# MLP: incoming items are normalised on ScalarE by scale and shift, and the first four are added and measured one by one

## The reference

```
x = x + attention_part(layernorm(x))
h0 = layernorm(x)                       # the incoming item, normalised: no weight, no bias
for blk in range(3):
    y = qlora_linear(h, first weights)
    y = gelu(layernorm(y) * gamma + beta)
    y = qlora_linear(y, second weights)
    h = y + h
x = x + h
```

## Time and profile before

| | |
|---|---|
| median of 3 runs | 1937.06 us (1936.43 to 1937.8) |
| profiled execution, its own time | 1935.07 us |
| its span | 1933.3 us |
| its mean TensorE clock | 0.972 of full speed |
| PE busy | 1806.9 us (93%) |
| DVE busy | 1434.5 us (74%) |
| ACT busy | 1311.9 us (68%) |
| POOL busy | 1184.4 us (61%) |
| `mlp_items` begins (first add, L1681) | 1526.6 us |

### The profile page before, as it was taken

How to read it: one execution, slowest core, us unless ns; L and a number is a source line. 1 busy time by engine, 2 the same in 40 slices (tenths; PEclk the granted TensorE clock), 3 DMA queues, 4 the chain that set the end, 5 groups by cost and what they waited for, 6 DMA issues and landing times. The chain is left out here.

```text
span 1933.3 us, 36509 instructions
## 1 busy us (share of the span) xinstructions
PE 1806.9 (93%) x12544; PEld 1375.2 (71%) x12544; DVE 1434.5 (74%) x3135; ACT 1311.9 (68%) x2317; POOL 1184.4 (61%) x1032
## 2 busy tenths in 40 slices
PE   5799999999999999999999999999995699999998
PEld 4577777766777777777776777777763478888887
DVE  4687778887878777777777777777762677777865
ACT  2777776677777775777677776777751177777775
POOL 2466666666666664555555555555542088888886
PEclk9899999999999998999999999999997599999999
DMA  4011111111111111111111111111012311212001
GB/s 144 23 39 39 39 38 38 49 55 43 41 40 38 38 39 39 39 39 39 44 53 51 38 43 38 38 38 38 27 35 69 109 66 42 90 45 88 23 23 45
DMA packets 87272, 91.97 MB, mean 48 GB/s; under 512 B 4928, under 2 KB 82448, under 8 KB 87184
## 3 DMA queue, kind: packets, MB, share of 16 engines
q1 hardware_dynamic: 79360, 79.46, 12.6%
q10 hardware_dynamic: 7824, 11.37, 2.4%
HBM read 57.26 MB, written 25.17 MB: 43 GB/s over the span
## 5 line engine op out<-in xcount | busy, mean ns | idle before, releaser
L860 POOL TENSOR_TENSOR L_xc<-L_xpad,L_vec 128x512 f32<-128x512 f32 x160 | 166.2, 1039 | 421.3 <-ACT L_xpad L659 394.1
L381 PE MATMUL L_front<-L_uhi,L_whi 128*128 128x512 f32 x576 | 247.3, 429 | 13.1 <-DVE L_xc L1078 8.3
L530 PE MATMUL L_mix<-L_wo,L_yg 128*128 128x256 f32 x1024 | 238.4, 387 | 3.2 <-POOL L_yg L852 3.2
L381 PE MATMUL L_front<-L_uhi,L_wlo 128*128 128x512 f32 x576 | 229.7, 399 | 0.0
L381 PE MATMUL L_front<-L_ulo,L_whi 128*128 128x512 f32 x576 | 229.6, 399 | 0.0
L1090 DVE TENSOR_TENSOR L_m<-L_dbank,L_gm 128x512 f32<-128x512 f32 x256 | 175.7, 687 | 69.3 <-ACT L_dbank L699 68.8
L852 POOL TENSOR_TENSOR L_yg<-L_yg,L_sz 128x512 f32<-128x512 f32 x128 | 164.2, 1283 | 85.9 <-DVE L_yg L1105 85.9
L530 PEld LDWEIGHTS L_mix<-L_wo,L_yg 128*128 128x128 f32 x1024 | 191.8, 192 | 34.7 <-issue 7.0
L659 ACT ACTIVATE L_xpad<-L_front,L_pbias 128x512 f32<-128x512 f32 x160 | 108.8, 681 | 132.4 <-PE L_front L381 131.6
L697 ACT ACTIVATE L_dbank<-L_dbank 128x512 f32<-128x512 f32 x256 | 148.8, 581 | 45.1 <-PE L_dbank L437 45.0
L487 PE MATMUL L_ybank<-L_m,L_dtx 128*64 128x128 f32 x2048 | 161.3, 284 | 5.5 <-DVE L_m L1090 5.4
(11 more groups left out here) (172 smaller groups left out, 4683.3 us busy)
## 6 DMA issues: line engine op xcount, KB each, us to landing
h<-L_hres SPq DMA_DIRECT2D x32, 512.0 KB, 3.0
L_hin<-in_x SPq DMA_DIRECT2D x16, 512.0 KB, 4.7
L_hres<-in_x SPq DMA_DIRECT2D x16, 512.0 KB, 3.9
L_cc<-L_xc ACTq DMA_DIRECT2D x64, 128.0 KB, 2.3
L_hin<-h SPq DMA_DIRECT2D x16, 512.0 KB, 4.7
L_hres<-h SPq DMA_DIRECT2D x16, 512.0 KB, 3.8
M_hin<-h SPq DMA_DIRECT2D x16, 512.0 KB, 4.6
M_xin<-in_x SPq DMA_DIRECT2D x16, 512.0 KB, 5.6
```

The costliest lines, as they stand in the source:

```text
L381: last = nc.tensor.matmul(to[:, :], ww[:, kd, tile * P:(tile + 1) * P], a[:, kd, :], start=i == 0, stop=i == len(passes) - 1)
L530: last = nc.tensor.matmul(mix[1 - s][:, (b % 2) * DM:(b % 2 + 1) * DM], yg[:, t, b * P:(b + 1) * P], wo[layer][:, t, :], start=t == 0, sto ...
L860: nc.gpsimd.tensor_tensor(xc[p][:, q, :].rearrange("p (b i) -> p b i", b=NB), xpad[:, q, :, 0:P], vector(layer, "conv_w", q * TAPS, 1).uns ...
```

## The change

`norm_in` leaves DVE for ACT. It no longer computes (v - mean) * rstd but v * rstd + shift0, so DVE makes -mean (`mean0`, one more 128x4 instruction in `in_moments`), and POOL makes shift0 (one more 128x4 instruction in `scale_in`). On ACT an item's four tiles are done in two halves, in two successive steps, right ahead of the gelu; PE waits for both halves. `scale_in` moves behind `block_scale` in POOL's step. The first four items are now added, measured and scaled one item a step, in steps -4 to -1, and normalised in steps -2 to 1. For later items the steps of `add_x`, `in_stats`, `in_moments` and `scale_in` are as before (3, 5, ... and 4, 6, ...), and `norm_in` stands at 6 and 7, 8 and 9, 10 and 11, 12 and 13.

```diff
+        mean0, shift0 = sb("mean0_", [P, NB]), sb("shift0_", [P, NB, 1])
...
 (PE, turn_in)
-                pe.wait_ge(n0_done, t + 1)
+                pe.wait_ge(n0_done, 2 * t + 2)
...
 (ACT)
+            def norm_in(t, half):
+                if t is None:
+                    return
+                u = t % UNITS
+                act.wait_ge(n0_shift, t + 1)
+                for b in (2 * half, 2 * half + 1):
+                    last = nc.scalar.activation(normed[u][:, b, :], held_by(t)[:, b, :], ACT.Identity, bias=shift0[u][:, b, :], scale=rstd0[u][:, b, :])
+                last.then_inc(n0_done, 1)
...
                 round_h(n, 1)
+                norm_in(entering(n, 2, 6), 0)
+                norm_in(entering(n, 2, 7), 1)
                 gelu(n - 2, 0)
...
 (POOL, scale_in)
                 nc.gpsimd.tensor_tensor(rstd0[u][:, :, 0], var0[u][:, :, 0], power[:, :], ALU.pow).then_inc(n0_rstd, 1)
+                pool.wait_ge(n0_rstd, t + 1)
+                pool.wait_ge(n0_mean, t + 1)
+                nc.gpsimd.tensor_tensor(shift0[u][:, :, 0], mean0[u][:, :], rstd0[u][:, :, 0], ALU.mult).then_inc(n0_shift, 1)
...
                 rest_h(n + 1, 1)
-                scale_in(entering(n, 2, 4))
                 block_scale(n)
+                scale_in(entering(n, 4, 4))
...
 (DVE, in_moments)
                 nc.vector.tensor_scalar(var0[u][:, :, 0], mv0[u][:, :, 1], EPS, None, ALU.add).then_inc(n0_var, 1)
-
-            def norm_in(t):
-                if t is None:
-                    return
-                u = t % UNITS
-                dve.wait_ge(n0_rstd, t + 1)
-                dve.wait_ge(n0_mom, NB * t + NB)
-                for b in range(NB):
-                    last = nc.vector.tensor_scalar(normed[u][:, b, :], held_by(t)[:, b, :], mv0[u][:, b, 0:1], rstd0[u][:, b, :],
-                                                   ALU.subtract, ALU.mult)
-                last.then_inc(n0_done, 1)
+                nc.vector.tensor_scalar(mean0[u][:, :], mv0[u][:, :, 0], -1.0, None, ALU.mult).then_inc(n0_mean, 1)
...
 (DVE, step)
-                norm_in(entering(n, 1, 5))
-                add_x(entering(n, 7, 3))
-                in_stats(entering(n, 2, 4), 0)
+                add_x(entering(n, 4, 3))
+                in_stats(entering(n, 4, 4), 0)
...
-                in_moments(entering(n, 2, 4))
+                in_moments(entering(n, 4, 4))
                 block_stats(n, 3)
```

More of the change, by code:

```diff
@@ L1422, in mlp_items @@
         b_mean, b_normed = sem("b_mean"), sem("b_normed")
+        n0_mean, n0_shift = sem("n0_mean"), sem("n0_shift")
         b_turned, b_gelu, g_hi, g_lo = (sem(n) for n in ("b_turned", "b_gelu", "g_hi", "g_lo"))
@@ L1750, in step @@
                 add_h(n - 3, 1)
-                norm_in(entering(n, 1, 5))
-                add_x(entering(n, 7, 3))
-                in_stats(entering(n, 2, 4), 0)
-                in_stats(entering(n, 2, 4), 1)
+                add_x(entering(n, 4, 3))
+                in_stats(entering(n, 4, 4), 0)
+                in_stats(entering(n, 4, 4), 1)
                 add_out(n - 3, 0)
@@ L1757, in step @@
                 block_stats(n, 0)
-                in_stats(entering(n, 2, 4), 2)
+                in_stats(entering(n, 4, 4), 2)
                 block_stats(n, 1)
-                in_stats(entering(n, 2, 4), 3)
+                in_stats(entering(n, 4, 4), 3)
                 block_stats(n, 2)
-                in_moments(entering(n, 2, 4))
+                in_moments(entering(n, 4, 4))
                 block_stats(n, 3)
```

## The result

The changed kernel takes 1941.12 us (median of 16 runs, 1937.96 to 1942.41) where the kernel before took 1934.62 us (16 runs, 1932.63 to 1939.13). The ratio is 1.0029, 95% interval 1.0021 to 1.0036: slower by 0.3%. I had forecast 1935.3 us and a range of 1927 to 1939; the time lies above the range. The forecast stood on the median of three runs, 1937.06 us; against the 16 runs its change of -1.8 us would be 1932.8 us, and the measured change is +6.5 us. The profiled execution has a span of 1939.9 us, 6.6 us more than before, at a mean clock of 0.971 (before 0.972).

A forecast was written before the change was run, and what follows sets the result against it. PE was taken as the bound, losing time to POOL's late low part of the gelu. Rounds -0.6 and start -1.2 gave -1.8 us, so 1935.3 us; range 1927 to 1939, leaving out 2 in 10.

The forecast's parts named there:

- The blocked mean: On DVE, `mean0` behind `var0` waits 1.27 us for POOL's second `rest_h`, delaying the slot's statistics and `var`.
- POOL's wait for the slot's `var`: On POOL, before the slot's power in steps 4, 6, 8, 10: idles about 1.1 us.
- `add_x` now falls on the new power, which lets it pass; only the small shift behind it waits, some 0.2 us instead of 1.0: DVE's add runs beside the incoming item's power on POOL; only shift0 is delayed, some 0.2 us.
- 0.2 to 0.4 behind `add_x`: Term in POOL's time for two steps: its waiting behind DVE's add, 0.2 to 0.4 us.
- the pair's sum: POOL's time for two steps: slots' work, item's power, shift0, idling and waiting behind `add_x`, 15.1 us against 15.61 before.
- the forecast of the rounds: Three rounds of entering items: PE loses 3.4 us each instead of 3.6, together -0.6 us.
- the path to PE: PE's `turn_normed` follows POOL's `rest_g` by about 0.4 us, so step 5 begins 1.1 us late.
- the power holds off `add_x`: Slower rival: `add_x` waits for the incoming power's end, +1.0 us on POOL in nine steps; +7, 1944 us; chance 0.06.
- "-1.2 us" at the start: First four items: slot 0's normalise begins 1.0 + 0.15 us earlier and ACT carries that on, -1.2 us.
- 0 if item 1's shift is held up by the next add: Bound on the start's gain: none if the next add (1.2 us) delays item 1's shift and the copy.
- ACT at no cost: ACT's halves of `norm_in`, about 1.0 us each, fit where it waits for `turn_normed`: cost zero, at most 0.5 us each.
- Nothing blocks `mean0`: Faster rival: `mean0` slips between POOL's two `rest_h`, the 1.1 us idling goes; -11.7, 1925.4 us; chance 0.24 with in-between cases.

The follow-up runs named there:

- experiment 1: The changed kernel with an incoming item's negative mean made by POOL behind the item's power, no longer by DVE: 1929.4 us, ratio 0.9975 to the kernel before.
- experiment 3: The changed kernel with `add_x` of items 4 to 15 moved behind the slot's first statistics: 1939.49 us, ratio 1.0022 to the kernel before.
- experiment 4: The changed kernel with `norm_in` of the first four items one step later on ACT: 1941.84 us, ratio 1.0039 to the kernel before.
- experiment 10: The changed kernel with DVE making `mean0` one step later, behind the slot's own variance and mean: 1926.78 us, ratio 0.9963 to the kernel before.
- Experiment 5: The changed kernel with the first four items' adds all ahead of the first statistics, as before: 1938.65 us, ratio 1.0017 to the kernel before.
- experiment 6: The changed kernel with the mean made by POOL and `scale_in` again ahead of `block_scale`: 1926.09 us, ratio 0.995 to the kernel before.
- experiment 9: The changed kernel with the mean on POOL, `scale_in` ahead of `block_scale` and the first four adds ahead of the first statistics: 1926.04 us, ratio 0.9961.
- experiment 7: The kernel before plus an unused `mean0` made by DVE behind `var0`, `norm_in` staying on DVE: 1949.99 us, ratio 1.0085.
- experiment 8: The kernel before with only `scale_in` moved behind `block_scale`: 1961.13 us, ratio 1.0135.
- experiment 2: The changed kernel with `scale_in` again ahead of `block_scale`: 1931.11 us, ratio 0.9981 to the kernel before.

## Why the prediction was wrong

**The blocked mean: right.** "`mean0` waits for the second `rest_h`: 1.27 us". It takes 1.32 or 1.33 for all twelve later items, and 0.16 for the first four. POOL's wait for the slot's `var`, forecast at 1.1, is 1.06. shift0 is 0.20 (0.24 forecast).

**The first step that failed: "`add_x` now falls on the new power, which lets it pass; only the small shift behind it waits, some 0.2 us instead of 1.0"**, the term "0.2 to 0.4 behind `add_x`" of the pair's sum. I took `add_x` to start behind the power. My own layout had the power at 1581.35 and the add at about 1581.4, and I did not ask what 0.1 us the other way would do. Measured: the add starts at 1581.53, the power at 1581.55 and takes 2.06. The term is 1.05, not 0.3. With it the pair is 12.4 + 2.06 + 0.24 + 1.06 = 15.8 us, as measured (15.83), against my 15.1, and 1.87 us are lost in three steps of a round instead of 1.1. That is 0.75 x 9 = 6.7 us in all, nearly the whole distance of 6.95 between the forecast of the rounds (-0.6) and the result (+6.35). Experiments 1, 3, 4 and 10 show the term, and so do all twelve traces together: in 78 cases an add starts while a power runs, and the power takes 1.0 us in each; in 47 it starts ahead of the power, which then takes 1.9 to 2.1. The idling and the path to PE were right; the order of the two starts, and with it the size of this term, was not. The row that I had gone by shows the one order only: in the earlier trace rows `norm_in` starts 0.40 us behind the power.

The rival that named this meeting ("the power holds off `add_x`") gave 1944 us, and had 6 in 100. The engines met, with the parts exchanged: the add held off the power. The price of about 1 us in nine steps was that of the rival, and so was the change, +7 us forecast and +6.5 measured; that it was right in size is luck, as its order did not occur. I had looked for evidence on one direction only,'s four tiles that pass beside a power, and none on the other. The Trainium skill's rule (SBUF — State Buffer, "Who interferes with whom": whoever issues first gets the shared pair for the whole instruction, the other is blocked) holds here where the add is first, 0.02 us ahead and the power 1.05 longer. It does not hold where the power is first: in experiment 1 the add starts 0.42 us into the power and takes its usual 1.22.

**The second: "-1.2 us" at the start.** It is +1.0. By the clock of the trace two signs look right: the first copy came at about the same time (1536.77), and slot 0's normalise 1.2 us earlier (1550.76 against 1551.95). But 0.72 of that is the earlier first add. Counted from the first add, the copy came 0.6 us later (10.90 against 10.27) and the normalise only 0.5 earlier (24.89 against 25.36), where I had 1.15 for it. What I called a bound ("0 if item 1's shift is held up by the next add") happened: the power took 1.98 us. The loss of 1.0 came behind, in `first_linear(1)` (4.86 us instead of 3.85) at a lower clock, for which the sum had no term. Experiment 5 shows that it goes with the adds one by one in this kernel; why the clock falls stays open.

**A slip in the range.** By its own terms (the start at -2.4, each round 0.7 less) the lower end of the main forecast is 1932.0, not 1932.5. It changes nothing here.

**ACT at no cost: right.** The gelus still wait for PE behind either half (1.81 and 0.28 us). In experiment 6 that wait is gone, so the cover is used up there; but the rounds take as long as in experiment 10, where the gelus still wait (51.67 and 51.65 us), so ACT is no bound there either.

**"Nothing blocks `mean0`": the forecast of what would happen then was right in kind.** I had put 1925.4 us on it; experiments 6, 9 and 10, where nothing blocks the mean or POOL has work meanwhile, take 1926.0 to 1926.8.

**What the change is made of.** Moving the normalising to ACT, with its order on POOL repaired, is worth 0.4 to 0.5% (experiments 6, 9 and 10). The mean behind `var0`, with the scale behind the slot's power and the add that then falls ahead of the item's power, gives more than all of it back. Its parts have no price that holds in every order: on the kernel before, the mean costs 0.85% and the moved scale 1.35% (experiments 7, 8), because there they push `norm_in` from a power onto the low parts.

## What to carry to other kernels

- Where VectorE and GpSimd both work in SBUF, look at what GpSimd does when a small VectorE instruction comes up; here one of 0.16 us took 1.32 beside GpSimd's subtractions. Try it where GpSimd has just run dry, or behind what GpSimd waits for: here the same instructions cost 14.1 us more over the three rounds in one place than in the other, where steps 4 to 11 take no longer (51.65 us) than with the mean on GpSimd and the scale ahead (51.67).
- If a forecast lets two instructions of two engines start within 0.1 us of each other, work out both orders, and give both a chance. A long add just ahead of a short power cost 1.05 us a time; begun 0.42 behind the power's start it cost 0.4.
- A part of a change that costs little in it can cost much more alone. Before judging a mixed change by its sum, look for the part that shields the others (here, that the four normalisings are gone from VectorE).

## What the runs showed of the hardware

- GpSimd's power of 128x4 takes 1.01 us whether a VectorE add of 128x1024 joins it on the way or not; the add takes 1.22 us beside it (78 cases in the twelve traces). When the add is ahead, by 0.02 us, the power takes 2.06 (1.9 to 2.1 in 47 cases). The meeting is not symmetrical. That the power needs its operands only at its beginning would explain it; no run here shows that.
- What GpSimd starts while such an add is still running waits, however small it is: 0.62, 1.03 and 1.27 us for instructions that take 0.20 to 0.23 us alone, with 0.5, 1.0 and 1.2 us of the add left (experiments 1, 3, 2).
- Four VectorE `tensor_scalar` of 128x256 take 1.37 us when they start 0.40 us into a power (its last 0.76 us; they end 0.6 behind it), and 5.34 us beside four GpSimd subtractions of 128x512 (experiment 7).
